# FFN's first four columns and weight slices moved into the last batch's heads, last modulation moved into the FFN

## What is computed

```python
    x = L0_attn_x
    xn = _layernorm(x, axis=-1)
    s = _L0_attn_ref(xn, ...)          # the state-space block
    g = _silu(_L0_ffn_ref(xn, ...))
    x = x + s * g
    return x
...
        # inside _L0_ffn_ref: D = 512, F_ = 2048, R = 16, 16 heads of 32
        x = _rmsnorm(hidden_states, ln1_w)
        attn = _attention(x, Wq, Wk, Wv, Wo)
        mod = MOD_SCALE * jnp.tanh(attn @ A)
        h = _rmsnorm(residual, ln2_w)
        gate_pre = h @ W_in_base.T + mod * (h @ A) @ B
        gate = jax.nn.silu(gate_pre)
        up = h @ W_up_base.T
        mlp_out = gate * up @ W_down.T
        return residual + mlp_out
```

## Time and profile before

| | |
|---|---|
| median of 3 runs | 2644.2 us (2637.21 to 2644.73) |
| the profiled execution: time / span | 2645.11 us / 2643.3 us |
| PE busy | 2507.3 us (95%), 14359 matmuls |
| DVE busy | 1405.5 us (53%) |
| ACT busy | 1072.3 us (41%) |
| POOL busy | 374.0 us (14%) |
| mean granted TensorE clock | 0.978 of full |

### The profile page before, as it was taken

One profiled execution on the slowest core, in us unless ns is written; L12 is line 12 of the kernel. 1 busy time (PEld: TensorE's weight loads), 2 busy tenths in 40 slices (PEclk: granted clock), 3 DMA queues, 4 the chain that ended last, 5 costly groups with the idle time before them and its releaser, 6 DMA issues.

```text
span 2643.3 us, 38302 instructions
## 1 busy us (share of the span) xinstructions
PE 2507.3 (95%) x14359; PEld 2019.0 (76%) x14359; DVE 1405.5 (53%) x2927; ACT 1072.3 (41%) x1776; POOL 374.0 (14%) x356
## 2 busy tenths in 40 slices
PE   4799999999999999999999979999999999999997
PEld 3678787787777777777777668888888788888886
DVE  6666566576664578888888752222213423333333
ACT  4444444445444367777777731111112211111111
POOL 0000000000000234444443300000000001111111
PEclk9899999999999999999999689999999999999999
DMA  4000000000002477666666321111112412222212
GB/s 137 16 17 17 32 1 32 32 1 33 17 1 99 140 222 201 187 177 188 161 178 184 121 72 48 48 48 48 48 48 96 143 39 94 96 96 96 96 61 79
DMA packets 106973, 228.13 MB, mean 86 GB/s; under 512 B 14976, under 2 KB 15488, under 8 KB 100624
## 3 DMA queue, kind: packets, MB, share of 16 engines
q1 hardware_dynamic: 106528, 225.34, 26.8%
q10 hardware_dynamic: 256, 0.26, 0.0%
HBM read 149.77 MB, written 75.50 MB: 85 GB/s over the span
## 4 chain that ended last, share of the span: by engine, by line
PE 85%; DVE 6%; issue 3%; ACT 3%; DMA 2%; SPq 0%; POOL 0%; DVEq 0%; ACTq 0%; POOLq 0%
PE PS L72 14%; PE PS L74 13%; PE PS L73 13%; PE PS L1939 4%; PE PS L1940 4%; PE PS L1941 4%; PE PS L1577 3%; PE PS L1596 3%; PE PS L1554 2%; PE PS L697 2%; PE PS L696 2%; PE PS L698 2%; PE PS L1556 2%; PE PS L1555 2%; PE PS L682 1%
## 5 line engine op out<-in xcount | busy, mean ns | idle before, releaser
L1988 DVE TENSOR_TENSOR GF<-SG,PS 128x512 f32<-128x512 f32 x128 | 88.0, 688 | 619.2 <-PE PS L74 619.2
L1728 DVE CUSTOM_DVE_ANT_0 PS<-PS,MK 128x512 f32<-128x512 f32 (+3 forms) x512 | 244.1, 505 | 94.7 <-PE PS L1577 93.5
L1962 ACT ACTIVATE SG<-PS 128x512 f32<-128x512 f32 x128 | 76.8, 600 | 430.0 <-PE PS L1921 429.9
L1677 ACT ACTIVATE PF<-PS 128x512 f32<-128x512 f32 (+1 forms) x384 | 200.0, 526 | 76.3 <-PE PS L1598 74.3
L1966 ACT CAST GH<-GF 128x512 fp32r<-128x512 f32 x128 | 79.4, 620 | 363.2 <-DVE GF L1988 363.2
L72 PE MATMUL PS<-XH,WH 128*128 128x512 f32 x512 | 211.4, 413 | 6.4 <-DVE XC L976 6.4
L2019 POOL TENSOR_SCALAR XN<-XT,MEAN,RSTD 128x512 f32<-128x512 f32 x32 | 68.3, 2136 | 1039.6 <-DMA M<-m_scratch 725.1
L72 PE MATMUL PS<-FH,GW 128*128 128x512 f32 x512 | 200.3, 391 | 7.8 <-DVE DW L1983 7.8
L1939 PE MATMUL PS<-DW,GH 128*128 128x512 f32 x512 | 200.3, 391 | 4.1 <-DVE GL L1990 4.1
L74 PE MATMUL PS<-XH,WL 128*128 128x512 f32 x512 | 202.7, 396 | 0.0
L73 PE MATMUL PS<-XL,WH 128*128 128x512 f32 x512 | 202.3, 395 | 0.0
(11 more groups left out here) (279 smaller groups left out, 5828.0 us busy)
## 6 DMA issues: line engine op xcount, KB each, us to landing
qk_scratch<-QT SPq DMA_DIRECT2D x128, 256.0 KB, 4.6
QS<-qk_scratch SPq DMA_DIRECT2D x96, 256.0 KB, 4.0
KS<-qk_scratch SPq DMA_DIRECT2D x96, 256.0 KB, 4.0
FH<-rh_scratch SPq DMA_DIRECT2D x16, 1024.0 KB, 6.0
FL<-rl_scratch SPq DMA_DIRECT2D x16, 1024.0 KB, 8.0
XF<-in_x_dram SPq DMA_DIRECT2D x32, 256.0 KB, 4.0
s_scratch<-ZS SPq DMA_DIRECT2D x8, 1024.0 KB, 5.9
rh_scratch<-RH SPq DMA_DIRECT2D x8, 1024.0 KB, 9.9
```

What stands on the lines that cost most here:

```text
L1677: act.activation(PE_[u][:, o:o + at], PS[4 + a % 2][:, 0:at], ACT.Exp, scale=SC).then_inc(a_ex, 1)
L1728: dve.tensor_tensor_reduce(out=p[:, at:at + n], in0=p[:, at:at + n], in1=MK[:, 512 - n:512], scale=1.0, scalar=NEG, op0=ALU.add, op1=ALU.m ...
```

## The change

The FFN's first four columns, all of batch 0, no longer stand in the FFN. Their gates and ups are steps of the attention list (`gate`, `up`, half of each at a time, six matmuls), in the last batch's thirds 349 to 385, in banks 1 and 0. Their silu is written as x/2·(1+tanh(x/2)): `bent` (ACT) and `gated`, `hidden` (DVE), then `hidden_high` (ACT) and `hidden_low` (DVE). The four weight slices that they need are scaled and split on POOL: 24 steps `part` at thirds 338 to 378, and 8 steps `part_down` at thirds 374 to 386. For this the FFN's buffers lie in memory that the projections leave (rows FH0 and FL0, slices GU0, hidden parts GH and GL, now four of each), and SP loads slices 0 and 1 ahead of the last `relay`, rows 0 and slice 2 behind it, then the four slices of the down weights, slice 3, and what the FFN needs next.

The sums of the last four heads and the last batch's modulation leave the attention list. The sums stand behind `slice` 4 on DVE, the modulation behind `column` 4, in bank 3. The FFN begins with `down` 0 and 1, then column 4; `down` 2 and 3 stand behind the modulation. A column's gate now waits for its own batch's modulation instead of all of them. The product is written over SG, so GF is gone. The semaphores of `relay` and `largest_out` are shared by four groups instead of one for each.

```diff
-                at(12 * w + 17, "inverse", w)
-                at(12 * w + 19, "divided", w)
-                at(12 * w + 20, "summed", w)
-                at(12 * w + 21, "gathered", w)
+                if w + 1 < 4 * NB:
+                    at(12 * w + 17, "inverse", w)
+                    at(12 * w + 19, "divided", w)
+                    at(12 * w + 20, "summed", w)
+                    at(12 * w + 21, "gathered", w)
             bank_of["modulation", b] = 0
-            at(t + 107, "modulation", b)
-            at(t + 108, "modulated", b)
-            at(t + 109, "modulation_out", b)
-            at(t + 110, "modulation_low", b)
...
+            if b + 1 < NB:
+                at(t + 107, "modulation", b)
+                at(t + 108, "modulated", b)
+                at(t + 109, "modulation_out", b)
+                at(t + 110, "modulation_low", b)
+
+        t = 3 * HEADS - 48
+        places = [third for third in range(t + 2, t + 48) if third % 3 != 1 and third % 12 != 5]
+        for n in range(EARLY):
+            for j in range(2):
+                for step in range(3):
+                    at(places.pop(0), "part", n, (j, step))
+        places = [third for third in range(t + 38, t + 60) if third % 3 != 1 and third % 12 != 5]
+        for n in range(EARLY):
+            for step in range(2):
+                at(places.pop(0), "part_down", n, step)
+        for q, (gate, up) in enumerate((((13, 14), (16, 17)), ((23, 24), (26, 27)), ((33, 34), (36, 37)), ((43, 44), (48, 49)))):
+            bank_of["gate", q], bank_of["up", q] = 1, 0
+            for half in range(2):
+                at(t + gate[half], "gate", q, half)
+                at(t + up[half], "up", q, half)
+            at(t + gate[1] + 1, "bent", q)
+            at(t + gate[1] + 2, "gated", q)
+            at(t + up[1] + 1, "hidden", q)
+            at(t + up[1] + 2, "hidden_high", q)
+            at(t + up[1] + 3, "hidden_low", q)
         at(-44, "factor", 0)
         at(-38, "factor_low", 0)
         steps = [w for third in sorted(thirds) for w in thirds[third]]
 
-        turn01, frees01 = {}, ([], [])
+        turn01, frees01 = {("modulation", NB - 1): (3, 0)}, ([], [])
...
+                    if a + 1 == 4 * NB and how == 1:
+                        load_slice(sp, 0)
+                        load_slice(sp, 1)
                     relay(sp, a, how)
...
+                elif kind in ("gate", "up"):
+                    if how == 0:
+                        own01(kind, a)
+                        pe.wait_ge(m_r[0], 32)
+                        pe.wait_ge(m_so, 2 * a + 2)
+                    p, x = bank01(kind, a), 2 * (kind == "up")
+                    for k in (2 * how, 2 * how + 1):
+                        c = slice(128 * k, 128 * k + 128)
+                        pe.matmul(p[:, :], GU[0][:, a, x, c], FH[0][:, k, :], start=k == 0, stop=False, skip_group_check=True)
+                        pe.matmul(p[:, :], GU[0][:, a, x, c], FL[0][:, k, :], start=False, stop=False, skip_group_check=True)
+                        t = pe.matmul(p[:, :], GU[0][:, a, x + 1, c], FH[0][:, k, :], start=False, stop=k == 3 and kind == "up",
+                                      skip_group_check=True)
+                    if how == 1 and kind == "up":
+                        t.then_inc(m_u, 1)
+                    elif how == 1:
+                        pe.wait_ge(a_th, 3)
+                        pe.wait_ge(a_mo, 2)
+                        pe.matmul(p[:, :], BS[:, 128 * a:128 * a + 128], MS[:, 0:S], start=False, stop=True,
+                                  skip_group_check=True).then_inc(m_g, 1)
...
+                elif kind == "bent":
+
+                    act.wait_ge(m_g, a + 1)
+                    if a >= 2:
+                        act.wait_ge(m_gl, a - 1)
+                    act.activation(SG[a % 2][:, :], bank01("gate", a)[:, :], ACT.Tanh, scale=0.5).then_inc(m_sg, 1)
+                elif kind == "hidden_high":
+                    act.wait_ge(m_gf, a + 1)
+                    act.wait_ge(a_rst, 32 * NB)
+                    act.wait_ge(a_qo[0], 128 * NB)
+                    act.wait_ge(a_qo[1], 128 * NB)
+                    act.copy(GH[a % 4][:, :], SG[a % 2][:, :]).then_inc(m_gh, 1)
                 elif kind == "modulation":
...
+                elif kind == "gated":
+                    sg = SG[a % 2][:, :]
+                    dve.wait_ge(m_sg, a + 1)
+                    dve.scalar_tensor_tensor(out=sg, in0=sg, scalar=1.0, in1=bank01("gate", a)[:, :], op0=ALU.add,
+                                             op1=ALU.mult).then_inc(m_ga, 1)
+                elif kind == "hidden":
+                    sg = SG[a % 2][:, :]
+                    dve.wait_ge(m_ga, a + 1)
+                    dve.wait_ge(m_u, a + 1)
+                    dve.scalar_tensor_tensor(out=sg, in0=sg, scalar=0.5, in1=bank01("up", a)[:, :], op0=ALU.mult,
+                                             op1=ALU.mult).then_inc(m_gf, 1)
+                elif kind == "hidden_low":
+                    dve.wait_ge(m_gh, a + 1)
+                    dve.tensor_tensor(GL[a % 4][:, :], SG[a % 2][:, :], f32(GH[a % 4][:, :]), ALU.subtract).then_inc(m_gl, 1)
...
+                elif kind == "part":
+                    j, step = how
+                    w, hi, lo = slice_parts(a)[j]
+                    if step == 0:
+                        pool.wait_ge(m_wf[a % 2], weights_landed(a))
+                        pool.tensor_tensor(w, w, l2b(), ALU.mult).then_inc(m_sl, 1)
+                    elif step == 1:
+                        if a == j == 0:
+
+                            pool.wait_ge(a_tr, 4 * NB)
+                            pool.wait_ge(a_lr, NB)
+                            pool.wait_ge(a_vl, 4 * NB)
+                            pool.wait_ge(a_pj, 8 * NB)
+                            pool.wait_ge(a_rst, 32 * NB)
+                        pool.wait_ge(m_sl, 2 * a + j + 1)
+                        pool.tensor_copy(hi, w).then_inc(m_sh, 1)
+                    else:
+                        pool.wait_ge(m_sh, 2 * a + j + 1)
+                        pool.tensor_tensor(lo, w, f32(hi), ALU.subtract).then_inc(m_so, 1)
+                elif kind == "part_down":
+                    if how == 0:
+
+                        pool.wait_ge(a_wt, 3 * HEADS - 12)
+                        pool.wait_ge(m_wd, 16 * EARLY)
+                        pool.tensor_copy(DW[:, a, 0, :], DST[:, a, :]).then_inc(m_dh, 1)
+                    else:
+                        pool.wait_ge(m_dh, a + 1)
+                        pool.tensor_tensor(DW[:, a, 1, :], DST[:, a, :], f32(DW[:, a, 0, :]), ALU.subtract).then_inc(m_do, 1)
...
+            yield "slice", 4
+            yield "sums", 4 * NB - 1
+            yield "slice", 5
+            yield "rows", 1
+            yield "down", 0
+            yield "down", 1
+            yield "column", 4
+            yield "modulation", NB - 1
+            yield "product", 4
+            yield "slice", 6
+            yield "down", 2
+            yield "down", 3
...
+                        if q > EARLY:
+                            yield "column", q
+                            yield "product", q
+                            if f or b:
+                                yield "down", q - 1
+                        if f == 0 and b and (half == 0 or b + 1 < NB) or q == 64:
                             yield "rows", 8 * half + b + 1
                         if half == 1 and 1 <= f <= 4 and b > 0:
...
+        def load_slice(sp, n):
+            u = n % 2
+            if n < 2:
+                sp.wait_ge(a_pj, 8 * NB)
+            else:
+                sp.wait_ge(m_so, slice_halves(n - 2))
+            sp.dma_start(STG3[u][:, 0, :], WgT[n]).then_inc(m_wf[u], 16)
+            sp.dma_start(STG3[u][:, 1, :], WuT[n]).then_inc(m_wf[u], 16)
+            if n >= EARLY:
+                sp.dma_start(STG3[u][:, 2, :], wd_[n]).then_inc(m_wf[u], 16)
+
...
+            sp.wait_ge(a_rst, 32 * NB)
+            load_rows(sp, 0)
+            load_slice(sp, 2)
+
+            sp.wait_ge(a_wt, 3 * HEADS - 36)
+            sp.wait_ge(a_qo[1], 128 * NB)
+            for n in range(EARLY):
+                sp.dma_start(DST[:, n, :], wd_[n]).then_inc(m_wd, 16)
+            load_slice(sp, 3)
             for kind, n in work:
...
+                    if q == 4:
+                        pe.wait_ge(m_gf, 4)
+                    elif q == 5:
+                        pe.wait_ge(m_ga, 4)
+                    else:
                         pe.wait_ge(m_sg, q - 1)```

PE, the last batch's first moved column, at thirds 349 and 350 (head 116). Before, the scores of one third follow those of the other:

```order
15047 L1577 MATMUL PS<-KS,QS 128x384
15048 L1577 MATMUL PS<-KS,QS 128x128
15049 L1596 MATMUL PS<-QS,KS 128x256
15050 L1598 MATMUL PS<-MR,idb 128x128
15051 L1577 MATMUL PS<-KS,QS 128x256
15052 L1596 MATMUL PS<-QS,KS 128x512
```

(27 more changed lines are left out.)

203 lines of the change are left out of this document (105 added, 98 removed).

## The result

The changed kernel takes 2632.05 us (median of 11 runs, 2628.17 to 2635.43) against 2643.99 us before: a ratio of 0.9959, 95% interval 0.9949 to 0.9968, so 11.9 us or 0.4% faster. I had forecast 24.9 us off the profiled execution. The direction was right and the size was not.

The account below looks back on a forecast made before the run. The FFN was taken as bound by PE alone, the last attention batch as slowed by a low clock, then a hole. Terms −22.7 − 14.0 + 1 + 10.8 = −24.9 us gave 2620.2 us from 2645.1, main case 2609 to 2630.

Parts of the forecast that it names:

- The 100 matmuls and the hole: FFN and PE's gap before it: 22.7 us off for moved matmuls, 14.0 off for the gap, 1 added for waits.
- Heads 117 to 121: Last batch: PE 4.55 us a head, DVE 4.4 with waits, taken as 5.0 a head, 25.0 us.
- DVE against POOL: Last batch: DVE waits for POOL's new instructions, 0.25 us for L1735 and 0.1 for sums and columns' low parts a head.
- heads 122 to 127: Last batch: PE leads alone at 3.97 us a head, taken as 4.1, 24.6 us.
- POOL's prices: POOL's 128x512 instructions: 1.15 us for two inputs, 0.8 for a copy; 24.8 us for the slices over 13.3 heads.
- rival B: POOL leads the last batch at 2.1 us an instruction, gates waiting for slices: 2631 us, up to 2640; chance 0.14.
- the last batch, summed: Heads 112 to 127: 21.5, 25.0 and 24.6 us, 71.1 instead of 60.3 to the last exponential, 10.8 us added.
- SP: Four DMAs ahead of the last relay: keys go out 1.7 us later, not needed before head 118; rows 0 there by 1476.
- rival C: Heads 117 to 127: the low clock stays at 0.50, 80.4 us instead of 49.6, so 2651 us; chance 0.07.
- The sum: Whole kernel: 24.9 us off the profiled 2645.1 us, giving 2620.2 us.
- The signs: Profile after: heads 117 to 127 clock near 1.00, PE over 95% busy; slice 4 within 5.5 us, last `mixed` near 1536.5.

Follow-up runs that it names:

- e11: Changed kernel with its real POOL instructions, slices 0 and 1 loaded one relay earlier and rows 0 ahead of the last relay: 2629.2 us.
- e10: Changed kernel with slices and rows 0 loaded earlier, POOL's 24 slice instructions replaced by about equally long memsets that read nothing, stand-in weights: 2622.4 us.
- e9: Changed kernel with slices and rows 0 loaded earlier, POOL's 24 slice instructions replaced by one-column memsets, stand-in weights coming by DMA: 2620.2 us.
- e4: Changed kernel with slices 0 and 1 loaded one relay earlier: 2630.6 us.
- e6: Changed kernel with POOL's 24 slice instructions as one-column memsets, stand-in weights by DMA, slices' loads one relay earlier, rows 0 not moved: 2628.4 us.
- e5: Changed kernel with slices 0 and 1 loaded one relay earlier and POOL's 24 slice steps begun one head earlier: 2627.3 us.

## Why the prediction was wrong in size, step by step

- **The 100 matmuls and the hole**, −22.7 − 14.0 + 1: measured −34.5 instead of −35.7. Right, the waits behind the hole too: slice 4 was 5.1 us on DVE instead of 4.7 (1549.43 + 0.69 to 1555.2), and column 4 waited 0.7 us for it.
- **Heads 117 to 121**, 25.0: 25.1 to 25.2 in every kernel that had the columns and POOL's steps at their old places, with POOL's work and without. PE's 4.55 us a head plus the friction of a full batch was a sound way to price them.
- **The step that failed** is "DVE against POOL", 0.35 us a head or 1.75 us in all, and charged in heads 112 to 116 alone. The reads of POOL's new work cost 6.8 us (e11 against e10; 6.2 us up to the last `mixed`). In heads 112 to 116 it is 3.1 us, 0.62 a head, about twice my term: DVE's low parts lost 0.34 us a head where I had 0.25, since two of the five met a difference on POOL with 0.9 and 1.3 us still to run, and the sums lost 0.32 where I had 0.1 with the columns' low parts in it. In heads 122 to 127 I had charged nothing, as PE leads there. The exclusion costs 3.0 us there (30.1 against 27.1), and not through DVE: POOL is later at slice 2. Head 123 takes 7.8 us instead of 5.3, PE waits 0.9 us at the gate, and the clock is at 0.50 for 3.4 us with PE 3.35 us busy, which costs half of it, 1.7 us by estimate.
- **POOL's prices**, 1.15 and 0.8 us: 1.18 for the scale, 1.56 for the difference (1.27 undisturbed) and 0.62 for the copy, so 26.8 us for the 24 instead of 24.8. Near enough, and rival B (2.1 us each) was not what happened. Yet its mechanism was: gates waited for slices, 3.4 us in two waits, because the last step of a slice is one third ahead of its gate and POOL ran 11 us without a gap ahead of slice 3's. I had compared mean loads (2.9 us of 4 to 5) and not the places. In heads 122 to 127 POOL is busy for 24.69 of 30.1 us. POOL's time alone, without reads, makes these heads 4.9 us longer (27.1 in e10, 22.2 in e9); the rest of the last batch gives about 4 of it back.
- **The first gate** was left out of "the last batch, summed". Its 13 matmuls stand at thirds 349 and 350, which is head 116, and I charged the columns to heads 117 to 127 only. Head 116 takes 8.2 us in e9 against 5.7 before; the 2.4 us that heads 122 to 127 came in below my sum there hide it in the sum.
- **SP**: I had the four DMAs in front of the last relay, and asked only who needs the keys. What needed the slices first was POOL, which stood at `part` 0 for 3 us with the low part of head 113 behind it. I had named "what is queued behind the waiting instruction" for PE and not for POOL. Its worth by itself is 1.1 us (e4), since DVE and POOL then collide instead. And I had counted only the time of issue: the keys went out at 1472.21, 7.1 us later than in the kernel before and not 1.7, behind a relay's store that took 6.1 us to land, and rows 0 were there at 1483.3 and not by 1476. In this kernel the first gate came at 1485.05, so that was luck; in e6 it cost 8.4 us.
- **The low clock**: rival C, in part. 27.3 us at 0.50 instead of 61.4, in three pieces. PE waited 2.5 us for POOL right ahead of the first, and two or three times for 0.3 to 0.9 us ahead of each of the others; each ended while 512-column matmuls ran, and it never stayed.
- **The sum**: from 2619.1 us (the forecast against the median before) to 2632.05 are 13 us. 1.1 of it is there without POOL's work (e9), 2.2 come with POOL's time (e10), 6.8 with its reads (e11), and 2.9 with the order of the loads (e11 against the changed kernel). The first, second and last are not clear of noise.
- **The signs**: the clock from head 122 to 127 was 0.77 on the mean, and PE was 90% busy in heads 117 to 121 and 79% in 122 to 127, not over 95%; slice 4 was done 6.1 us behind the last `mixed`, not 5.5; and the last `mixed` stood at 1548.9. The 1536.5 and 1081 given for it don't follow from my sum, which makes 1535.9 and 1082.5.

## What to carry to other kernels

Work moved to an idle engine must be priced in the place where it stands in that engine's queue: what is behind it there, what it needs to have landed, and how many steps lie between its last instruction and the one that waits for it. A mean load of 60 to 80% says nothing about it; in this kernel a slack of one third was too little, and five or six were enough (e5). GpSimd is not idle room beside a VectorE that has two SBUF inputs: what it reads is paid for by both engines.
